# Selective scan: state products summed four at a time on GpSimd before TensorE accumulates them, a product ring of six, and row selection over all 128 partitions

## What is computed

```
x = x + 0.5 * ffn_fp4(layernorm(x))         # b lane
x = x + mamba(layernorm(x))                 # a lane, two blocks
x = x + 0.5 * ffn_fp4(layernorm(x))         # b lane
x = x + 0.5 * moe(layernorm(x))             # c lane, 8 experts of 512
x = x + attention(layernorm(x))             # b lane, 16 heads of 8
x = x + 0.5 * moe(layernorm(x))             # c lane
```

```
deltaA  = exp(delta[..., None] * A)
deltaBx = delta[..., None] * Bm[:, :, None, :] * u[..., None]
h = deltaA * h + deltaBx                    # along the tokens
y = einsum('ben,bn->be', h, C)              # sum over the 16 states
y = (y + Dp * u) * silu(z)
```

## Time and profile before

| | |
|---|---|
| three runs | 2872.39, 2872.73, 2875.82 us; median 2872.73 |
| the profiled execution | 2876.84 us |
| its span, first to last instruction | 2875.1 us |
| mean granted TensorE clock | 0.953 of full |
| TensorE busy | 2733.4 us, 95% |
| VectorE busy | 1946.4 us, 68% |
| ScalarE busy | 1606.0 us, 56% |
| GpSimd busy | 1371.3 us, 48% |

### The profile page before, as it was taken

The page is one execution under the profiler, slowest core; times in us unless marked ns, Lnnn a source line. Parts: engine busy times, 40 slices in busy tenths (PEclk is TensorE's granted clock), DMA queues, the critical chain, the costliest instruction groups (busy, mean ns, idle before and its releaser), DMA issues.

```text
span 2875.1 us, 41563 instructions
## 1 busy us (share of the span) xinstructions
PE 2733.4 (95%) x14913; PEld 1895.2 (66%) x14913; DVE 1946.4 (68%) x3753; ACT 1606.0 (56%) x3405; POOL 1371.3 (48%) x1226
## 2 busy tenths in 40 slices
PE   7999999999999989999799899999999999999888
PEld 7777875786577655666366566656575666678675
DVE  5868887697868687676867886687858666432320
ACT  2433436435664556656486556756675676465654
POOL 2448475563737365454716474274636635311111
PEclk9999999999999989799799999999999999999899
DMA  4223122131213021211202121121202112000000
GB/s 147 67 67 104 55 64 74 45 92 42 79 40 96 23 73 39 70 49 49 77 20 78 37 76 31 49 70 31 75 19 86 36 52 67 1 4 1 1 5 4
DMA packets 88573, 150.60 MB, mean 52 GB/s; under 512 B 10565, under 2 KB 21485, under 8 KB 88110
## 3 DMA queue, kind: packets, MB, share of 16 engines
q1 hardware_dynamic: 88366, 147.94, 16.4%
HBM read 145.26 MB, written 2.65 MB: 51 GB/s over the span
## 4 chain that ended last, share of the span: by engine, by line
PE 83%; ACT 7%; DVE 5%; POOL 3%; issue 2%; DMA 0%; POOLq 0%; SPq 0%; ACTq 0%; DVEq 0%
PE c_bank L912 16%; PE c_bank L920 16%; PE c_bank L1338 13%; PE a_bank L758 8%; PE a_bank L748 5%; PE b_bank L1072 3%; PE b_bank L1061 3%; PE a_bank L727 2%; PE b_bank L1085 2%; PE b_bank L1084 2%; PE b_bank L582 1%; PE b_bank L563 1%; PE b_bank L565 1%; PE b_bank L1083 1%; PE a_bank L764 1%
## 5 line engine op out<-in xcount | busy, mean ns | idle before, releaser
L829 POOL TENSOR_TENSOR prod_c<-hst,prod_c 128x512 f32<-128x512 f32 x512 | 666.0, 1306 | 502.0 <-DVE hst L706 478.1
L706 DVE TENSOR_TENSOR_SCAN hst<-dA,a_bank 128x512 f32<-128x512 f32 x512 | 621.0, 1213 | 16.3 <-ACT dA L818 6.8
L912 PE MATMUL c_bank<-c_xT,w 128*128 128x512 f32 x1024 | 544.3, 638 | 7.7 <-ACT weighted_y L955 4.7
L818 ACT ACTIVATE dA<-delta,a_neg 128x510 f32<-128x510 f32 x512 | 364.2, 718 | 330.8 <-DVE hst L706 325.4
L920 PEld LDWEIGHTS c_bank<-w,hid 128*128 128x128 f32 x4096 | 491.2, 193 | 80.0 <-issue 47.5
L920 PE MATMUL c_bank<-w,hid 128*128 128x128 f32 x4096 | 529.4, 281 | 3.1 <-ACT hid L947 3.1
L1338 PEld LDWEIGHTS c_bank<-ident 128*128 128x128 f32 x3752 | 449.1, 193 | 66.4 <-issue 60.4
L1338 PE MATMUL c_bank<-ident 128*128 128x128 f32 x3752 | 483.4, 281 | 0.5 <-ACT weighted_y L955 0.4
L947 ACT ACTIVATE hid<-c_bank,b 128x512 f32<-128x512 f32 x512 | 349.7, 687 | 185.2 <-PE c_bank L912 183.5
L700 DVE TENSOR_TENSOR a_bank<-du,a_bank 128x512 f32<-128x512 f32 x512 | 350.5, 685 | 132.7 <-PE a_bank L748 128.5
L971 POOL TENSOR_TENSOR xs<-xs,weighted_y 128x512 f32<-128x512 f32 x128 | 167.9, 1312 | 544.6 <-ACT weighted_y L955 544.0
(11 more groups left out here) (179 smaller groups left out, 3550.8 us busy)
## 6 DMA issues: line engine op xcount, KB each, us to landing
prod_c<-c_rows SPq DMA_DIRECT2D x512, 256.0 KB, 3.1
w<-in_w SPq DMA_DIRECT2D x2, 2048.0 KB
xs<-in_x SPq DMA_DIRECT2D x8, 256.0 KB, 8.6
bias<-skew SPq DMA_DIRECT2D x1, 2048.0 KB, 8.8
out_dram<-xs SPq DMA_DIRECT2D x8, 256.0 KB, 2.3
in_wT<-in_in_wT SPq DMA_DIRECT2D x1, 512.0 KB
c_rows<-bcC SPq DMA_DIRECT2D x16, 32.0 KB, 1.6
b_hq<-in_w_gu SPq DMA_DIRECT2D x1, 384.0 KB, 3.2
```

What stands on the lines that cost most here:

```text
L706: nc.vector.tensor_tensor_scan(hst[:, s % RS, :], dA[:, s % RA, :], b_bank, 0.0, ALU.mult, ALU.add).then_inc(M.h.sem, 1)
L818: nc.scalar.activation(half_batches(dA[:, s % RA, :], 1), half_batches(delta[:, h, :], 1), ACT.Exp, scale=a_neg[:, l, h, n:n + 1]).then_in ...
L829: nc.gpsimd.tensor_tensor(prod[:, s % RP, :], hst[:, s % RS, :], cring[:, s % RC, :], ALU.mult).then_inc(M.pp.sem, 1)
L912: nc.tensor.matmul(S.bank[up_bank(e, c)][:, :], w1[:, e, c * 128:(c + 1) * 128], S.xT[:, :], start=True, stop=True).then_inc(M.up.sem, 1)
```

## The change

Three things change in the mamba block.

- GpSimd adds once more: after every fourth step it adds two pair sums, so that the slot of the first product holds a sum of four. TensorE accumulates these, 4 for each half in place of 8. Its sum stands after the selection of step 4k + 6. The skip term of the first half moves from after scan step 19 to after scan step 21.
- The product ring grows from four slots to six. GpSimd's product of step s >= 6 waits for sum (s - 6) // 4 + 1.
- The selection reads all 128 partitions of `sel` and `bc3`. Partitions 0 to 63 are zero in both: GpSimd clears `bc3` once at the start and fills `sel` from `eye2`, whose rows 0 to 63 are zero. The values are the same.

All order strings are new. In them TensorE has 1907 spares in place of 1876, and 128 sums in place of 256. GpSimd has 929 steps of lane a in place of 801. The numbers of the other steps are the same.

```diff
@@ -35,90 +35,86 @@
 MAGIC = 1.5 * 2.0 ** 22
 BELOW = 1.0 - 2.0 ** -24
 XR = 6
-RS, RA, RP, RC = 3, 3, 4, 4
+RS, RA, RP, RC = 3, 3, 6, 4
 
 
 ORDER_PE = (
-    "b2d8bd41bd3b2d6b2d6b2d27bd3b3d37b6d55adba3b2d9b2ad5ab2a2d8ad17bd13adb2d3bdad7ad28a2d3ad8adad10ad12a2d8ad14a2"
+    "b2d8bd37bd3b2d6b2d6b2d28bd3b3d38b6d57aba3b2d9b2ad5ab2a2d5ad26ad3bd8b3ad5ad27ad7ad8ad10a2d7ad12ad13ad4ad4ad7a"
 ...
 ORDER_POOL = (
-    "ab5a2b2a13ba86bab2a18ba12ba13ba5cab2aca7ca6ca9ca6ca6ca6ca3ca6bab2a18ba12ba13ba5cab2aca6baca3ba3ba3ca5ca6ca3c"
+    "ab5a2b2a16ba99bab2a9ba7ba11ba3ca10ba11ba6c2a5ca7ca4ca7ca7ca3ca25bab2a9ba7ba11ba3ca10ba11ba5bab2caca4ca7ca7c"
 ...
 
 
 def merge(order, lanes, spare=None):
@@ -353,7 +349,8 @@
                 self.h = sig(n + "_state", STEPS, use, uses)
                 self.pp = sig(n + "_product", STEPS, use, uses)
                 self.pair = sig(n + "_product_pair", STEPS // 2, use, uses)
-                self.sum = sig(n + "_state_sum", STEPS // 2, use, uses)
+                self.quad = sig(n + "_product_quad", STEPS // 4, use, uses)
+                self.sum = sig(n + "_state_sum", STEPS // 4, use, uses)
                 self.yD = sig(n + "_y_with_skip", 2, use, uses)
                 self.y = sig(n + "_y", 2, use, uses)
                 self.proj = sig(n + "_out_product", 1, use, uses)
@@ -647,6 +644,8 @@
                                                op0=ALU.add, op1=ALU.mult).then_inc(M.sz.sem, 1)
                 yield
             dve.wait_ge(M.cE.sem, L.at(M.cE, 1))
+            if l == 0 and L.g == 0:
+                dve.wait_ge(s_const, 3 + RA)
             nc.vector.scalar_tensor_tensor(out=bcr[64:128, :], in0=bch[64:128, :], scalar=cut3[64:128, 0:1], in1=S.bank[2][64:128, :],
                                            op0=ALU.mult, op1=ALU.add).then_inc(M.bcR.sem, 1)
             yield
@@ -682,7 +681,7 @@
                 yield
 
             def half_end(h):
-                dve.wait_ge(M.sum.sem, L.at(M.sum, (h + 1) * NST // 2))
+                dve.wait_ge(M.sum.sem, L.at(M.sum, (h + 1) * NST // 4))
                 nc.vector.scalar_tensor_tensor(out=yT[:, h, :], in0=u[:, h, :], scalar=chan[:, 1, l, h:h + 1],
                                                in1=S.bank[1][:, :], op0=ALU.mult, op1=ALU.add).then_inc(M.yD.sem, 1)
                 yield
@@ -708,7 +707,7 @@
                 yield
                 if s == 1:
                     yield from softplus_end(1)
-                if s == NST + 3:
+                if s == NST + 5:
                     yield from half_end(0)
             yield from half_end(1)
             dve.wait_ge(M.proj.sem, L.at(M.proj, 1))
@@ -739,24 +738,24 @@
                                  start=True, stop=True).then_inc(M.dt.sem, 1)
                 yield
             pe.wait_ge(M.bcS.sem, L.at(M.bcS, 1))
-            for s in range(STEPS + 4):
+            for s in range(STEPS + 3):
                 if s < STEPS:
                     if s == 1:
                         pe.wait_ge(M.delta.sem, L.at(M.delta, 1))
                     elif s:
                         pe.wait_ge(M.h.sem, L.at(M.h, s - 1))
-                    nc.tensor.matmul(S.bank[2 - s % 2 * 2][:, :], sel[64:128, s % NST, :], bc3[64:128, :],
+                    nc.tensor.matmul(S.bank[2 - s % 2 * 2][:, :], sel[:, s % NST, :], bc3[:, :],
                                      start=True, stop=True).then_inc(M.b.sem, 1)
                     yield
-                if s >= 4 and s % 2 == 0:
-                    k = s // 2 - 2
-                    pe.wait_ge(M.pair.sem, L.at(M.pair, k + 1))
+                if s >= 6 and s % 4 == 2:
+                    k = s // 4 - 1
+                    pe.wait_ge(M.quad.sem, L.at(M.quad, k + 1))
                     if k == 0:
                         pe.wait_ge(M.delta.sem, L.at(M.delta, 2))
-                    if k == NST // 2:
+                    if k == NST // 4:
                         pe.wait_ge(M.yD.sem, L.at(M.yD, 1))
-                    nc.tensor.matmul(S.bank[1][:, :], ident[:, :], prod[:, 2 * k % RP, :],
-                                     start=(k % (NST // 2) == 0), stop=(k % (NST // 2) == NST // 2 - 1)).then_inc(M.sum.sem, 1)
+                    nc.tensor.matmul(S.bank[1][:, :], ident[:, :], prod[:, 4 * k % RP, :],
+                                     start=(k % (NST // 4) == 0), stop=(k % (NST // 4) == NST // 4 - 1)).then_inc(M.sum.sem, 1)
                     yield
             pe.wait_ge(M.y.sem, L.at(M.y, 2))
             for t in range(TT):
@@ -824,7 +823,7 @@
             for s in range(STEPS):
                 pool.wait_ge(s_c[s % RC], 16 * (i * STEPS // RC + s // RC + 1))
                 if s >= RP:
-                    pool.wait_ge(M.sum.sem, L.at(M.sum, s // 2 - 1))
+                    pool.wait_ge(M.sum.sem, L.at(M.sum, (s - RP) // 4 + 1))
                 pool.wait_ge(M.h.sem, L.at(M.h, s + 1))
                 nc.gpsimd.tensor_tensor(prod[:, s % RP, :], hst[:, s % RS, :], cring[:, s % RC, :],
                                         ALU.mult).then_inc(M.pp.sem, 1)
@@ -833,6 +832,11 @@
                     pool.wait_ge(M.pp.sem, L.at(M.pp, s + 1))
                     nc.gpsimd.tensor_tensor(prod[:, (s - 1) % RP, :], prod[:, (s - 1) % RP, :], prod[:, s % RP, :],
                                             ALU.add).then_inc(M.pair.sem, 1)
+                    yield
+                if s % 4 == 3:
+                    pool.wait_ge(M.pair.sem, L.at(M.pair, s // 2 + 1))
+                    nc.gpsimd.tensor_tensor(prod[:, (s - 3) % RP, :], prod[:, (s - 3) % RP, :], prod[:, (s - 1) % RP, :],
+                                            ALU.add).then_inc(M.quad.sem, 1)
                     yield
 
         c_dram = a["c_rows"]
@@ -1179,7 +1183,7 @@
                 for l in range(LAYERS):
                     if g == 0 and l == 0:
                         act.wait_ge(m_ready, 4)
-                        act.wait_ge(s_const, 2 + RA)
+                        act.wait_ge(s_const, 3 + RA)
                     if l == 0:
                         act.wait_ge(mam_ln.out.sem, L.at(mam_ln.out, 1))
                     else:
@@ -1192,11 +1196,12 @@
                 nc.gpsimd.memset(dA[:, b, :], 0.0).then_inc(s_const, 1)
             nc.gpsimd.memset(vx[:, :, :, DH:DH + 1], 1.0).then_inc(v_ones, 1)
             pool.wait_ge(v_ones, 1)
-            pool.wait_ge(s_const, 1 + RA)
+            nc.gpsimd.memset(bc3[:, :], 0.0).then_inc(s_const, 1)
+            pool.wait_ge(s_const, 2 + RA)
             pool.wait_ge(s_wm, 16 * len(load_m))
-            nc.gpsimd.tensor_copy(sel[64:128, :, :], eye2[64:128, :].unsqueeze(2).to_broadcast([64, NST, 128])).then_inc(s_const, 1)
-            yield
-            pool.wait_ge(s_const, 2 + RA)
+            nc.gpsimd.tensor_copy(sel[:, :, :], eye2[:, :].unsqueeze(2).to_broadcast([128, NST, 128])).then_inc(s_const, 1)
+            yield
+            pool.wait_ge(s_const, 3 + RA)
             for g in range(GROUPS):
                 L.g = g
                 yield from rstd_pool(pool, L, sa, mam_ln.stats, mam_ln.rstd)
...
```

150 lines of the change are left out of this document (73 added, 77 removed).

## The result

The changed kernel took **2780.31 us** (median of four runs, 2776.03 to 2789.25), beside 2874.28 us for the kernel before on the same chip: a ratio of 0.9669, interval 0.9635 to 0.9704. That is 94 us less, where 109 were forecast, and inside the range. The sum came near, but by luck: two of its terms were wrong by 100 us or more in opposite directions, as the experiments show.

The account below looks back on a forecast made before the run. The prediction took the scan loop to set the pace early and TensorE's list in the long dense part. Terms -128 + 8 + 5 + 6 = -109 us gave 2764 us against the runs' median, range 2722 to 2840.

Parts of the forecast that it names:

- Selection over 128 rows: 0: TensorE's selection: same 404 ns expected as with 64 rows, so 0 us; bounds 0 and 51 us lost.
- selections above 404 ns: Sign listed as showing the forecast wrong: TensorE's selections lasting longer than the 404 ns mean of before.
- Sums removed: -128 us: TensorE: 128 of 256 sums go, at 1.0 us each; -128 us, bounds 110 and 147.
- TensorE's other idle time and its time at 1.2 GHz are taken to stay: Assumption behind the total: TensorE's remaining idle time and its time at the lower clock don't change.
- the first three blocks at no gain and no loss: Up to the third block's last selection: 85 more spares (22 us) offset 23 fewer sums (23 us).
- Spares, +8: TensorE's order: 31 more spares at 0.26 us each, adding 8 us.
- Adds on GpSimd, hidden: GpSimd: 171 us of added work, 10.7 us a block, covered by 31 us a block of idle time before products.
- later sums: TensorE's waits for sums: half as many, 14, but 2.4 us each; +5 us, bounds -14 and +40.
- the shared memory: VectorE and GpSimd contending at SBUF: losses grow by 12 us, half on the path; +6 us, bounds 0 and 24.
- The ring of six, 0: GpSimd's product ring: it waited only 19.3 us for sums and has slack, so 0 us.
- Rival 3: TensorE has room; select, multiply and scan set the pace throughout and freed time is idle: 2885 us, chance 0.05.
- rival 4: Less array work lets the clock fall, doubling the time at 1.2 GHz: +135, so 2899 us, chance 0.04.

Follow-up runs that it names:

- e11: Kernel before with the selection over 128 rows and a product ring of six, keeping pair sums and its own order: ratio 0.9657, 2778.71 us.
- e5: Kernel before with only the selection changed, to read all 128 rows: ratio 0.9647, 2778.87 us.
- e1: Changed kernel with the selection back on 64 rows, all else as changed: ratio 1.0025, 2889.21 us.
- e9: Kernel before with 128 of its 256 sums on 8 of 512 columns, leaving out part of y: ratio 0.9983, 2876.26 us.
- e6: Changed kernel without the third add; TensorE makes two pair sums at each place of a sum of four: ratio 0.9889, 2849.04 us.
- e3: Changed kernel's code with the orders of the kernel before, every other sum struck out, 1876 spares: ratio 0.9927, 2862.44 us.
- e2: Changed kernel with GpSimd's third add on 8 of 512 columns, so y is incomplete: ratio 0.9606, 2768.0 us.
- e4: Changed kernel with a product ring of four in place of six: ratio 0.9949, 2868.99 us.
- e12: Changed kernel with every spare on 96 rows in place of 128: ratio 0.9679, 2786.05 us.
- e7: Changed kernel with every spare on 64 rows in place of 128: ratio 0.9923, 2857.84 us.

## Why the prediction was right, and where it was not

The time was right, and by luck: two of its steps were wrong by 100 us or more each, in opposite directions.

Below, TensorE's busy time is split in two. In the stretches at 1.2 GHz a pass of a spare takes 213 ns from start to start, at 2.4 GHz 112. So half of the time for which TensorE is busy in the former is lost to the clock; the rest of its busy time is array work at full speed. The kernel before has it busy for 233 of 270 us at 1.2 GHz, e11 for 211 of 246, the changed kernel for 250 of 345.

**"Selection over 128 rows: 0", bounds 0 and a loss of 51 us: the step that failed.** e5 shows -102 us (0.0353), e1 the same with the opposite sign (+103). The step looked at the selection's duration and asked only whether the weight load would get longer. It did, from 92 to 98 ns in the median, and that doesn't show. What was there to be read is the start of the *next* matmul: in the trace of before, spares start 112 ns apart, but 208 ns before a selection and 213 ns behind the first one after it. I excluded a gain with no row for it. The sign that was to show this step wrong, selections above 404 ns, came true at 408 in the mean and meant nothing. The pieces, from e11's page against that of before: TensorE's busy time fell by 120 us, of which (233 - 211) / 2 = 11 us because less of it was at 1.2 GHz, and 109 us as array time, beside the bound of 129 from the changes; its idle time grew from 142 to 163 us.

**"Sums removed: -128 us" and "TensorE's other idle time and its time at 1.2 GHz are taken to stay": the second sentence failed.** From e11 to the changed kernel TensorE's busy time falls by 2613.8 - 2536.3 = 77.5 us, while (250 - 211) / 2 = 19.5 us of time come on top through the clock: 97 us of array work gone. The sum had -128 + 8 = -120 for it; at the lower bound of 0.86 us a sum it would have been -110 + 7 = -103, so the midway value of 1.0 us was too large. Then the idle time grew from 162.8 to 241.3 us, 78.5 more. Together, -97 + 19.5 + 78.5, they make the span's change of +1.0 us. So of 97 us freed none was left, 0.9669 beside e11's 0.9657: four fifths became waits, and one fifth went to the clock. In e9, where order and waits were left alone, it was the clock that took all. This account adds up two profiles; it doesn't say which wait brings which fall of the clock.

**Where the sums of four win and lose.** From the ends of the scans: the first eight blocks end at 1065 us in e5 and at 1144 in the changed kernel, the next eight take 1288 and 1212 us. The prediction had the first three blocks at no gain and no loss; they cost 34 us, and blocks four to eight another 45. Part of that is the order, which puts other work there: with pair sums in the new order (e6) the first eight end at 1181 us.

With 128 rows and a ring of six all four pairings were run: pair sums in the old order 0.9657 (e11), sums of four in the old order 0.9927 (e3), pair sums in the new order 0.9889 (e6), sums of four in the new order 0.9669. The new order without sums of four costs 67 us, sums of four without the new order 78, and both together 3, within the intervals. So neither has a price of its own, and a term for the sums that is added to the others could not hold.

**Spares, +8: wrong for a reason above.** They take 20 us less, because a run of them no longer begins and ends beside a matmul of 64 rows: with the same 1876 spares as before, e11 has 467.9 us for them in place of 483.4.

**Adds on GpSimd, hidden: right in the main.** GpSimd's busy time grew by 175 us (171 forecast). e2 puts their price at 12 to 18 us, beside the +5 and +6 of the forecast for later sums and the shared memory. The steps in the second block are 2.24 us apart (2.3 forecast), and uneven. VectorE there:

```profile
242.73 1.22 DVE L705 TENSOR_TENSOR_SCAN hst<-dA,a_bank 128x512 f32<-128x512 f32 x1
...
244.57 1.22 DVE L705 TENSOR_TENSOR_SCAN hst<-dA,a_bank 128x512 f32<-128x512 f32 x1
...
248.27 1.22 DVE L705 TENSOR_TENSOR_SCAN hst<-dA,a_bank 128x512 f32<-128x512 f32 x1
250.96 0.70 DVE L699 TENSOR_TENSOR a_bank<-du,a_bank 128x512 f32<-128x512 f32 x1 [1.47 <-PE a_bank L747]
251.69 1.22 DVE L705 TENSOR_TENSOR_SCAN hst<-dA,a_bank 128x512 f32<-128x512 f32 x1
```

Three of four steps take 1.84 us and the fourth 3.4, in which VectorE waits for the selection behind 15 spares and the sum.

**Later sums, +5: inside its bounds.** TensorE waits 46.0 us for GpSimd at the sum's line, loads and matmuls together, where it waited 28.3: 18 more. Of these 15 come with the row count, as e11, with pair sums, has 43.2. But this holds only for the new order: in the old one it is 99 us at the matmul alone (e3).

**The ring of six, 0: wrong as a part, right beside what was there.** With sums of four it is worth 81 us (e4), with pairs nothing (e11). It was costed by the waits of before, in which a slot is free after two steps and not after four.

**Rivals.** Rival 3's mechanism came true for the larger part (freed time is idle; its sign was 250 us of idle time, and it is 241), rival 4's for a smaller (the clock falls), each for the sums alone; I gave them 0.05 and 0.04 because I took TensorE's share of the chain, 83%, as proof that a microsecond off its list is one off the time. The rule of the Trainium skill (Perfetto Trace Analysis, Identifying the Most-Contended Engine), which judges TensorE by its weight loads, would have said rightly for the sums that nothing is won; for the row count it would have said the same, and there 102 us were. Neither the 95% of busy time nor the 66% of weight loads shows these gaps; the starts do. The range's inner bounds were a choice as well: the terms' bounds add up to 2720 and 2835 us without the selection's 51, not to 2722 and 2810.

**A simpler kernel.** Among the runs that compute all of y, none is faster than the changed kernel by more than the intervals. e5 has the changed kernel's time with one edit, the old order, a ring of four and 128 adds fewer on GpSimd. I would take it.

**Open.** Why a change of height costs 0.3 us; how the 78 us of idle time divide between the new order and the later sums; why a freed array lowers the clock in one order more than in another; and the attention's matmuls of 24 rows, which still pay (205 ns from a full pass to one of them, and 213 ns behind the first full pass after them, against 112 and 109). Padding them was not tried.

## What to carry to other kernels

When matmuls of different heights alternate, measure from the start of one to the start of the next, for each pair of kinds: durations and busy time hide what a change of height costs, and rows of zeros up to the full height can be the cheapest 100 us in a kernel. Time freed on a busy engine is a gain only if something fills it: test it alone, by shortening the operation, before an order is rebuilt around it. And undo each part of a change by itself: here one part of three made the whole gain, and the other two, with the order made for them, brought nothing.

## What the runs showed of the hardware

- A matmul with 64 rows between taller ones costs 0.3 us of TensorE: about 0.1 us on its own start (208 against 112 ns), 0.1 on the next one's (316 against 216) and 0.1 on the one after that (213 against 109). Matmuls of 24 and 8 rows pay too (205 ns behind a full 128-column pass for 24 rows, at each of the four start partitions; 533 against 429 for the second full 512-column start behind 8 rows). 96 rows (e12) and 65 count as full. Within a run of matmuls of 64 rows nothing is lost (112 ns a pass, e7), and a run of them loses 0.4 us in all.
- A bf16 weight load of 128 rows took 98 ns in the median and 107 in the mean, one of 64 rows 92 and 93, so twice the height made 6 to 14 ns.
- Array work taken away without a replacement was answered by a lower granted clock: 0.953 to 0.918 over the span in e9, and 0.92 to 0.87 in one dense stretch. 94 us of full-speed work went, 95 us were lost at 1.2 GHz, and the time stayed.
- Spares of 64 rows in place of full ones went with 0.924 in place of 0.938 (e7), spares of 96 rows with 0.934 (e12).
